# Expert tiles: the next expert's weights are rounded and split piece by piece under the last tile's products, and the gated rows go ahead of the output weights

## Chip, core and metric

The kernel runs on one core of a Trainium2 chip. The metric is the device time of one execution in microseconds (us), as the median of several runs; the profile is one further execution, recorded by the hardware profiler.

## What is computed

A block of four steps on `x` (16 sequences of 128 rows, width 512), each added to x with a `tanh` gate: a gated cross attention, a ternary linear layer, a sigmoid attention, and a mixture of experts. The change is in the last one. Cut to what matters there (T = 2048 tokens, E = 16 experts, 4 of them for each token, inner width 352):

```
_, idx = top_k(masked_scores, 4)                    # per token
cw = zeros(T, E).at[arange(T)[:, None], idx].add(w) # routing weights
h = silu(einsum('td,edh->teh', xf, w1)) * einsum('td,edh->teh', xf, w3)
y = einsum('teh,ehd,te->td', h, w2, cw)
z = silu(xf @ sw1) * (xf @ sw3) @ sw2               # shared experts
return (y + z).reshape(b, s, d)
```

## The kernel before

The steps before the experts, the routing and the shared expert fill the first 793 us and are left as they are. In `expert_tiles` the routed rows lie sorted by expert in tiles of 128 rows; 68 tiles are in use here. All engines run the same loop over trips of `UT` = 4 tiles (b = 0 to 3, n = 4 i + b). At the head of a trip each engine loads from the table `meta` whether the trip is in use and whether its first tile begins a new expert; in each tile it loads the flag of the next tile (`this, first = first, value_load(...)`). Such a load is a few register instructions and a TENSOR_LOAD in the engine's queue.

Products are made in three passes over values kept as a rounded high part (fp32r) and a low part (value minus high part). ScalarE rounds, VectorE subtracts.

TensorE, in tile n, issues in this order:
- the first products (L1925): for each of four pieces k of the width it waits for the low part of W13's piece (`w13_lo`), then six matmuls into `t_H1` and `t_H3`; the first waits for the low part of the rows, `tx_lo`;
- the transposes of the next tile's rows into `t_TX` (L1904);
- the second products of tile n-1, nine matmuls into `t_Y` (L47 to L49, `y(b)`), after waits for `th_lo` (gated rows), `w2_lo` (W2) and `y_evac`;
- the transposes of the gated rows into `t_TH` (L1937), after `hmul`.

ScalarE, in tile n: silu of `t_H1` (L1970), rounding of the next rows (L1947, `x_hi`), if the next tile has a new expert its W13 in four pieces (L1951), the output rows of tile n-1 times their routing weight (L1954, `y_out`), if this tile has a new expert its W2 in two parts (L1985, L1986), and rounding of the gated rows (L1991). VectorE: the routing weight column (L2022), the gated product (L2024), low part of the next rows (L1999, `x_lo`), W13's four splits (L2003), W2's two splits (L2039, L2042), low part of the gated rows (L2048). Where a branch for new weights isn't taken, the engine takes an Else with `drain()`, which waits until the engine is empty, and a semaphore increment in the splits' place.

W13 is one buffer: the pieces for tile n+1 overwrite those of tile n, so they can start only when tile n's products with them are through. Before the change one semaphore, `h_fill`, says so, at the end of all 24 matmuls. The raw weights have two places; SP loads the expert after the next (L1033, L1038, L1039) when a place has been split (`w13_lo`, `w2_lo`). GpSimd gathers rows (L1044) three tiles ahead and scatters the output rows with an add (L1893).

Twelve experts have rows in this input, so W13 changes eleven times inside the loop, and W2 is taken up twelve times. The tiles whose successor begins an expert are those at 801.49, 808.87, 844.27, 953.65, 988.34, 1009.77, 1037.81, 1045.81, 1101.49, 1163.03 and 1224.75 (start of L1904 in the profile).

## Time and profile before

| what | value |
|---|---|
| median of 3 runs | 1286.46 us (1286.46 to 1287.14) |
| span of the profiled execution, first to last instruction | 1286.6 us |
| TensorE matmul busy | 1210.8 us, 94% |
| VectorE busy | 676.6 us, 53% |
| ScalarE busy | 578.8 us, 45% |
| GpSimd busy | 424.5 us, 33% |
| mean granted TensorE clock | 0.986 of full speed |
| first to last tile start in the expert loop | 801.49 to 1266.07 us |
| load of half an expert's W13 (704 KB), issue to landing | 5.3 us, median |

Times in the views are in us from the start of the span. A busy share counts matmuls as they are modelled by the profiler, so 94% is no measure of the work done, but gaps in it are real. The profiled execution's only time is its span; what lies before the first and after the last instruction isn't in it.

### The profile page before, as it was taken

The numbers are of one execution on the slowest core, as the hardware profiler recorded it, in microseconds if no ns is written. First come the engines' busy times: TensorE is split into PE (matmuls) and PEld (weight loads), VectorE is DVE, ScalarE is ACT, GpSimd is POOL, SyncE is SP. The second block draws the span as 40 slices with busy tenths as digits, with TensorE's granted clock in tenths as the row PEclk, the third lists the DMA queues.
The fourth block names the chain that finished last, engine by engine and source line by source line (L and its number), as shares of the span: only waits on it lengthen the run. The fifth ranks groups of instructions, "written<-read, shape, count | busy, mean of one in ns | idle before, by whom it ended". The sixth has DMA issues, their size and how long they took to land. (4 is left out here: it accounts for less than half of the span.)

```text
span 1286.6 us, 25693 instructions
## 1 busy us (share of the span) xinstructions
PE 1210.8 (94%) x7835; PEld 1023.1 (80%) x7836; DVE 676.6 (53%) x1411; ACT 578.8 (45%) x1387; POOL 424.5 (33%) x514
## 2 busy tenths in 40 slices
PE   7998999999999879889999998999999999999995
PEld 7877777787787657667777777889999889999995
DVE  6656545545445989944576554642234552424241
ACT  5554445455356768872111112543344453434341
POOL 1102211211213656400015742244434334443443
PEclk9999999999999999989999999999999999999997
DMA  9100000000000122022000413764445766545454
GB/s 334 39 18 20 18 1 20 18 1 18 18 18 2 34 69 65 29 96 85 1 0 2 160 41 130 221 142 85 78 103 117 201 144 146 137 85 136 86 135 71
DMA packets 54335, 100.36 MB, mean 78 GB/s; under 512 B 5094, under 2 KB 21990, under 8 KB 54262
## 3 DMA queue, kind: packets, MB, share of 16 engines
q0 software_dynamic: 15824, 37.76, 15.5%
q1 hardware_dynamic: 38438, 61.65, 14.7%
q8 instruction: 43, 0.70, 0.2%
q14 instruction: 30, 0.25, 0.1%
HBM read 72.91 MB, written 26.48 MB: 77 GB/s over the span
## 5 line engine op out<-in xcount | busy, mean ns | idle before, releaser
L1925 PE MATMUL t_H<-m_W,t_xT 128*128 128x352 f32 x1632 | 281.9, 328 | 7.3 <-DVE m_W L2003 5.7
L1925 PEld LDWEIGHTS t_H<-m_W,t_xT 128*128 128x128 f32 x1632 | 263.3, 189 | 10.1 <-DVE m_W L2003 8.1
L1893 POOL DMA_INDIRECT out_dram<-t_ys,t_sid x68 | 109.5, 1610 | 225.0 <-ACT t_ys L1954 110.6
L1970 ACT ACTIVATE t_sl<-t_H 128x352 f32<-128x352 f32 x68 | 31.6, 465 | 175.6 <-PE t_H L1925 175.6
L759 ACT ACTIVATE pr<-SC,neg 128x128 f32<-128x128 f32 x256 | 90.1, 377 | 38.2 <-DVE neg L973 38.2
L47 PE MATMUL t_Y<-m_W,t_hT 128*128 128x512 f32 (+1 forms) x207 | 88.1, 426 | 4.9 <-issue 3.0
L2048 DVE TENSOR_TENSOR t_hT<-t_TH,t_hT 128x384 fp32r<-128x384 f32 x68 | 37.8, 556 | 101.8 <-ACT t_hT L1991 100.6
L2024 DVE TENSOR_TENSOR t_h<-t_H,t_sl 128x352 f32<-128x352 f32 x68 | 35.6, 523 | 104.8 <-ACT t_sl L1970 104.8
L1954 ACT ACTIVATE t_ys<-t_Y,t_wcol 128x512 f32<-128x512 f32 x69 | 47.4, 687 | 95.3 <-PE t_Y L49 95.3
L49 PE MATMUL t_Y<-m_W,t_hT 128*128 128x512 f32 (+1 forms) x207 | 82.5, 398 | 0.0
L48 PE MATMUL t_Y<-m_W,t_hT 128*128 128x512 f32 (+1 forms) x207 | 82.2, 397 | 0.0
L470 POOL TENSOR_TENSOR X<-X,upd 128x512 f32<-128x512 f32 x16 | 20.6, 1290 | 138.3 <-DVE upd L954 138.3
L697 ACT ACTIVATE pT<-T 128x512 f32<-128x512 f32 x64 | 38.5, 603 | 53.8 <-PE T L503 53.7
L970 DVE TENSOR_REDUCE mx<-SC 128x4 f32<-128x512 f32 x64 | 43.9, 686 | 33.7 <-PE SC L631 33.7
L1238 POOL TENSOR_SCALAR m_W<-m_W,bst 128x128 fp32r<-128x128 f32 x64 | 49.6, 795 | 31.4 <-PE eL L1353 31.2
L894 DVE TENSOR_TENSOR Wq<-kT,Wq 128x512 fp32r<-128x512 f32 x64 | 56.2, 902 | 3.7 <-ACT Wq L750 3.6
L440 POOL TENSOR_TENSOR tmp<-tmp,nhalf 128x2 f32<-128x2 f32 (+2 forms) x22 | 19.1, 870 | 117.3 <-DVE tmp L790 100.3
L1434 ACT ACTIVATE ehT<-eh 128x512 fp32r<-128x512 f32 (+1 forms) x24 | 15.2, 632 | 91.6 <-DVE eh L1720 91.6
L759 ACT ACTIVATION_READ_ACCUMULATOR pr<-SC,neg 128x1 f32 x256 | 55.3, 216 | 0.0
L1884 POOL COPY t_sid<-m_vals 128x1 uint32 x68 | 50.9, 748 | 0.5 <-issue 0.5
L47 PEld LDWEIGHTS t_Y<-m_W,t_hT 128*128 128x128 f32 (+1 forms) x207 | 39.4, 190 | 13.7 <-issue 5.3
L1999 DVE TENSOR_TENSOR t_xT<-t_TX,t_xT 128x512 fp32r<-128x512 f32 x69 | 47.6, 690 | 3.1 <-ACT t_xT L1947 0.3
(508 smaller groups left out, 3216.8 us busy)
## 6 DMA issues: line engine op xcount, KB each, us to landing
m_raw<-in_L_ffn_w_dram SPq DMA_DIRECT2D x28, 704.0 KB, 5.3
m_raw<-in_L_ffn_w_dram SPq DMA_DIRECT2D x14, 512.0 KB, 6.8
CT<-in_ctx_dram SPq DMA_DIRECT2D x8, 512.0 KB, 3.7
X<-in_x_dram SPq DMA_DIRECT2D x4, 1024.0 KB, 13.4
rows_d<-rows_first SPq DMA_DIRECT2D x16, 256.0 KB, 2.0
out_dram<-X SPq DMA_DIRECT2D x3, 1024.0 KB, 4.3
m_raw<-in_L_ffn_w_dram SPq DMA_DIRECT2D x14, 192.0 KB, 6.7
CT<-in_ctx_dram SPq DMA_DIRECT2D x8, 256.0 KB, 2.7
```

Source lines behind the costliest of these rows:

```text
L47: pe.matmul(out, lhs(0), rhs(0), start=first, stop=False)
L48: pe.matmul(out, lhs(0), rhs(1), start=False, stop=False)
L49: return pe.matmul(out, lhs(1), rhs(0), start=False, stop=last)
L759: i = act.activation(pr[:, t % 2, slot, :], SC[t % 2][:, slot * S:(slot + 1) * S], ACT.Exp, scale=SCALE0, bias=neg[:, t % 2, slot:slot + 1 ...
L894: dve.tensor_tensor(as_[:, n, 1, :], asg[:, n, :], as_[:, n, 0, :].bitcast(F32), ALU.subtract).then_inc(as_lo, 1)
L970: dve.tensor_reduce(mx[:, t % 2, :], bk, AX.X, ALU.max).then_inc(s_out, 1)
L1238: i = pool.tensor_scalar(tab_a[t % SLOTS][:, k, :], iP.bitcast(F32), place_p[:, t, k:k + 1], None, ALU.is_equal)
L1884: pool.tensor_copy(sid[:, b:b + 1], m["target"][:, bass.ds(n, 1)]).then_inc(zeroed, 1)
L1893: pool.indirect_dma_start(out=m["out_rows"][:, :], out_offset=bass.IndirectOffsetOnAxis(ap=sid[:, b:b + 1], axis=0), in_=ys[:, b, :], in_o ...
L1925: x_ = pe.matmul(bk[b % 2][:, 0:I], xT[:, b % 2, jx, k, :], W13[:, jw, k, j, :], start=k == 0 and jx == jw, stop=k == KC - 1 and jx == 1)
L1954: act.activation(ys[:, (b - 1) % UT, :], Y[(b - 1) % 2][:, :], ACT.Copy, scale=wcol[:, (b - 1) % UT:(b - 1) % UT + 1]).then_inc(y_evac, 1)
L1999: dve.tensor_tensor(xT[:, b % 2, 1, :, :], TX[:, :].rearrange("p (k t) -> p k t", k=KC), xT[:, b % 2, 0, :, :].bitcast(F32), ALU.subtract) ...
```

## The change

The semaphore `h_fill`, once per tile, becomes `h_part`, once per piece of the first products. ScalarE rounds pieces 0 to 2 of the next expert's W13 each behind the six matmuls that still read that piece, and only then does the gated steps (silu and rounding of the next rows, now `gated`), then piece 3. VectorE likewise: splits of pieces 0 to 2, gated product and low rows, split of piece 3. Where the next tile keeps its expert, the gated steps stand in the Else branch, ahead of its drain. Second, the rounding and the low part of the gated rows (`t_hT`) go ahead of the W2 branch on both engines, and so ahead of its drain where it isn't taken.

```diff
@@ tensor
-                            x_.then_inc(h_fill, 1)
+                                x_.then_inc(h_part, 1)
@@ scalar
+                def w13_k(k, place):
+                    act.activation(W13[:, 0, k, :, :], raw13(m, place)[:, k, :, :], ACT.Copy).then_inc(w13_hi, 1)
+                def gated(n, b):
+                    act.wait_ge(h_part, KC * n + KC)
+                    act.wait_ge(hmul, n + 1)
+                    act.activation(sl[:, :], H1[b % 2][:, 0:I], ACT.Silu).then_inc(silu, 1)
+                    act.wait_ge(tx_fill, n + 2)
+                    x_hi(b + 1)
...
-                            act.wait_ge(h_fill, n + 1)
-                            act.wait_ge(hmul, n + 1)
-                            act.activation(sl[:, :], H1[b % 2][:, 0:I], ACT.Silu).then_inc(silu, 1)
-                            act.wait_ge(tx_fill, n + 2)
-                            x_hi(b + 1)
                             with act.If(first):
                                 act.wait_ge(r13_in, 32 * (n + 2))
-                                w13(weights_at(act, m, n + 1))
+                                there = weights_at(act, m, n + 1)
+                                for k in range(KC - 1):
+                                    act.wait_ge(h_part, KC * n + k + 1)
+                                    w13_k(k, there)
+                                gated(n, b)
+                                w13_k(KC - 1, there)
                             with act.Else():
+                                gated(n, b)
                                 act.drain()
                                 act.sem_inc(w13_hi, KC)
                             act.wait_ge(y_fill, n + 1)
                             act.wait_ge(scattered, n + 1)
                             y_out(b)
+                            act.wait_ge(th_fill, n + 1)
+                            act.activation(hT[:, 0, :, :], TH[...], ACT.Copy).then_inc(th_hi, 1)
                             with act.If(this):
...
-                            act.wait_ge(th_fill, n + 1)
-                            act.activation(hT[:, 0, :, :], TH[...], ACT.Copy).then_inc(th_hi, 1)
@@ vector
+                def gated(n, b):
+                    dve.wait_ge(silu, n + 1)
+                    dve.tensor_tensor(h[:, 0:I], H3[b % 2][:, 0:I], sl[:, :], ALU.mult).then_inc(hmul, 1)
+                    dve.wait_ge(tx_hi, n + 2)
+                    x_lo(b + 1)
...
-                            dve.wait_ge(silu, n + 1)
-                            dve.tensor_tensor(h[:, 0:I], H3[b % 2][:, 0:I], sl[:, :], ALU.mult).then_inc(hmul, 1)
-                            dve.wait_ge(tx_hi, n + 2)
-                            x_lo(b + 1)
                             with dve.If(first):
                                 there = weights_at(dve, m, n + 1)
-                                for k in range(KC):
+                                for k in range(KC - 1):
                                     dve.wait_ge(w13_hi, 4 * (n + 1) + k + 1)
                                     w13_k(k, there)
+                                gated(n, b)
+                                dve.wait_ge(w13_hi, 4 * (n + 1) + KC)
+                                w13_k(KC - 1, there)
                             with dve.Else():
+                                gated(n, b)
                                 dve.drain()
                                 dve.sem_inc(w13_lo, KC)
+                            dve.wait_ge(th_hi, n + 1)
+                            dve.tensor_tensor(hT[:, 1, :, :], TH[...], hT[:, 0, :, :].bitcast(F32), ALU.subtract).then_inc(th_lo, 1)
                             with dve.If(this):
...
-                            dve.wait_ge(th_hi, n + 1)
-                            dve.tensor_tensor(hT[:, 1, :, :], TH[...], hT[:, 0, :, :].bitcast(F32), ALU.subtract).then_inc(th_lo, 1)
```

## Rows read from the trace of the kernel before

**Rows 1.** Timeline: start us, us, engine, line, operation [idle before <-releaser]; tile starts.

```profile
801.49 0.60 PE L1904 MATMUL t_TX<-identF,m_first 128*128 128x128 f32 x4
...
808.87 0.60 PE L1904 MATMUL t_TX<-identF,t_later 128*128 128x128 f32 x4
...
816.39 0.60 PE L1904 MATMUL t_TX<-identF,t_later 128*128 128x128 f32 x4
...
1266.07 0.60 PE L1904 MATMUL t_TX<-identF,m_first 128*128 128x128 f32 x4
```

**Rows 2.** Waits, 800 to 1286: waiter <- releaser: us in total, times, longest.

```profile
PEld t_H L1925 <- DVE m_W L2003: 8.1, 10, 1.3
...
PEld t_Y L47 <- issue: 5.3, 10, 3.2
...
PEld t_Y L47 <- DVE m_W L2042: 2.3, 3, 0.9
```

**Rows 3.** Timeline, an undisturbed tile with no new weights.

```profile
1142.81 0.60 PE L1904 MATMUL t_TX<-identF,t_later 128*128 128x128 f32 x4
...
1145.54 0.69 ACT L1954 ACTIVATE t_ys<-t_Y,t_wcol 128x512 f32<-128x512 f32 x1 [1.49 <-PE t_Y L49]
1145.59 4.13 PE L1925 MATMUL t_H<-m_W,t_xT 128*128 128x352 f32 x24
1146.34 0.49 ACT L1991 ACTIVATE t_hT<-t_TH 128x384 fp32r<-128x384 f32 x1
1146.87 0.56 DVE L2048 TENSOR_TENSOR t_hT<-t_TH,t_hT 128x384 fp32r<-128x384 f32 x1 [2.10 <-ACT t_hT L1991]
1147.68 0.15 DVE L2022 COPY t_wcol<-m_wgt 128x1 f32 x1 [0.26 <-issue]
...
1149.55 0.60 PE L1904 MATMUL t_TX<-identF,t_later 128*128 128x128 f32 x4
...
1149.75 0.47 ACT L1970 ACTIVATE t_sl<-t_H 128x352 f32<-128x352 f32 x1 [2.92 <-PE t_H L1925]
```

**Rows 4.** ScalarE's queue in that tile: L1988 and L1967: ns min/median/max, first, last start.

```profile
L1988 ACTq DRAIN  x1: 566/566/566, 1145.7 to 1145.7; - x1
...
L1967 ACTq SEQ_ASSERT  x1: 18/18/18, 1146.9 to 1146.9; - x1
```

**Rows 5.** Timeline, a tile whose successor has new weights.

```profile
953.65 0.60 PE L1904 MATMUL t_TX<-identF,t_later 128*128 128x128 f32 x4
...
954.29 0.60 ACT L1947 ACTIVATE t_xT<-t_TX 128x512 fp32r<-128x512 f32 x1
...
955.27 2.83 ACT L1951 ACTIVATE m_W<-m_raw 128x704 fp32r x4 [0.38 <-issue]
...
956.22 3.30 DVE L2003 TENSOR_TENSOR m_W<-m_raw,m_W 128x704 fp32r<-128x704 f32 x4 [0.61 <-ACT m_W L1951]
...
961.11 0.60 PE L1904 MATMUL t_TX<-identF,m_first 128*128 128x128 f32 x4
```

**Rows 6.** Timeline, VectorE at the head of a trip of four tiles.

```profile
1163.06 0.15 DVE L2022 COPY t_wcol<-m_wgt 128x1 f32 x1 [2.16 <-issue]
```

**Rows 7.** Timeline, W2 taken up in the last tile of a trip.

```profile
965.67 0.61 ACT L1986 ACTIVATE m_W<-m_raw 96x512 fp32r x1
...
969.40 0.15 DVE L2022 COPY t_wcol<-m_wgt 128x1 f32 x1 [1.18 <-issue]
...
969.90 0.68 DVE L1999 TENSOR_TENSOR t_xT<-t_TX,t_xT 128x512 fp32r<-128x512 f32 x1
...
970.88 0.41 PE L1925 MATMUL t_H<-m_W,t_xT 128*128 128x352 f32 x1
```

**Rows 8.** Timeline, the first trip: a load's issue and VectorE's first copy.

```profile
799.14 0.99 SPq L1033 DMA_DIRECT2D m_raw<-in_L_ffn_w_dram  x2
...
799.56 0.15 DVE L2022 COPY t_wcol<-m_wgt 128x1 f32 x1 [3.74 <-issue]
```

**Rows 9.** DMA queues, 793 to 1287: packets, MB, share of 16 engines.

```profile
q14 instruction: 4, 0.03, 0.0%
```

More of the change, by code:

```diff
@@ L1816, in expert_tiles @@
         r13_in, r2_in, w13_hi, w13_lo, w2_hi, w2_lo = (sem(f"t_{n}") for n in ("r13_in", "r2_in", "w13_hi", "w13_lo", "w2_hi", "w2_lo"))
-        tx_fill, tx_hi, tx_lo, h_fill, silu, hmul, th_fill, th_hi, th_lo, y_fill, y_evac, scattered = (
-            sem(f"t_{n}") for n in ("tx_fill", "tx_hi", "tx_lo", "h_fill", "silu", "hmul", "th_fill", "th_hi", "th_lo",
+        tx_fill, tx_hi, tx_lo, h_part, silu, hmul, th_fill, th_hi, th_lo, y_fill, y_evac, scattered = (
+            sem(f"t_{n}") for n in ("tx_fill", "tx_hi", "tx_lo", "h_part", "silu", "hmul", "th_fill", "th_hi", "th_lo",
                                     "y_fill", "y_evac", "scattered"))
@@ L1947, in x_hi @@
                     act.activation(xT[:, b % 2, 0, :, :], TX[:, :].rearrange("p (k t) -> p k t", k=KC), ACT.Copy).then_inc(tx_hi, 1)
-                def w13(place):
-                    for k in range(KC):
-                        act.activation(W13[:, 0, k, :, :], raw13(m, place)[:, k, :, :], ACT.Copy).then_inc(w13_hi, 1)
+                def w13_k(k, place):
[6 more added lines that the diff above has]
+                    x_hi(b + 1)
                 def y_out(b):
@@ L1981, in _ @@
                             y_out(b)
+                            act.wait_ge(th_fill, n + 1)
+                            act.activation(hT[:, 0, :, :], TH[:, 0:3 * P].rearrange("p (k t) -> p k t", k=3), ACT.Copy).then_inc(th_hi, 1)
                             with act.If(this):
@@ L1989, in _ @@
                                 act.sem_inc(w2_hi, 2)
-                            act.wait_ge(th_fill, n + 1)
-                            act.activation(hT[:, 0, :, :], TH[:, 0:3 * P].rearrange("p (k t) -> p k t", k=3), ACT.Copy).then_inc(th_hi, 1)
                 act.wait_ge(y_fill, trips * UT + 1)
@@ L2022, in _ @@
                             dve.tensor_copy(wcol[:, b:b + 1], wgt[:, bass.ds(n, 1)])
-                            dve.wait_ge(silu, n + 1)
-                            dve.tensor_tensor(h[:, 0:I], H3[b % 2][:, 0:I], sl[:, :], ALU.mult).then_inc(hmul, 1)
-                            dve.wait_ge(tx_hi, n + 2)
-                            x_lo(b + 1)
                             with dve.If(first):
                                 there = weights_at(dve, m, n + 1)
-                                for k in range(KC):
+                                for k in range(KC - 1):
                                     dve.wait_ge(w13_hi, 4 * (n + 1) + k + 1)
                                     w13_k(k, there)
+                                gated(n, b)
+                                dve.wait_ge(w13_hi, 4 * (n + 1) + KC)
+                                w13_k(KC - 1, there)
                             with dve.Else():
+                                gated(n, b)
                                 dve.drain()
                                 dve.sem_inc(w13_lo, KC)
+                            dve.wait_ge(th_hi, n + 1)
+                            dve.tensor_tensor(hT[:, 1, :, :], TH[:, 0:3 * P].rearrange("p (k t) -> p k t", k=3),
+                                              hT[:, 0, :, :].bitcast(F32), ALU.subtract).then_inc(th_lo, 1)
                             with dve.If(this):
@@ L2046, in _ @@
                                 dve.sem_inc(w2_lo, 2)
-                            dve.wait_ge(th_hi, n + 1)
-                            dve.tensor_tensor(hT[:, 1, :, :], TH[:, 0:3 * P].rearrange("p (k t) -> p k t", k=3),
-                                              hT[:, 0, :, :].bitcast(F32), ALU.subtract).then_inc(th_lo, 1)
 _INS = ['x', 'ctx_2048', 'mask_BxS2_bk0', 'g_xattn', 'g_ffn', 'L0_xattn_norm_w', 'L0_xattn_wq', 'L0_xattn_wk',
```

## Prediction

> **What bounds the kernel now.** I read the page's shares first (the table above): TensorE is busy nearly all of the span, so time can only come out of its gaps, or go into them. The change touches the expert tiles, the last third. There each tile starts with four transposes at L1904; 68 such starts lie between 801.49 and 1266.07 [rows 1], 67 intervals in 464.6 us. An undisturbed tile takes 1149.55 - 1142.81 = 6.74 us, product after product [rows 3]. 67 times 6.74 is 451.6, so all that can be won in this stage is 13.0 us. The view of waits says what these 13 us are [rows 2]: ten starts of the first products late by 8.1 us for the low part of the new expert's weights; three starts of the second products late by 2.3 us for W2's low part; and the "issue" row, 5.3 less the 3.2 of the very last tile, 2.1 us in nine tiles in which the low part of the gated rows came last. These sum to 12.5; the rest is two small delays.
>
> **Part 1: pieces split ahead.** Today the next expert's W13 is rounded on ScalarE after the gated rows: in the tile at 953.65 the pieces start at 955.27, VectorE follows at 956.22, the products wait for its first piece, and the tile takes 961.11 - 953.65 = 7.46 [rows 5], 0.72 over. Naively three pieces now run under the products and 8.1 us are gone. But the silu, the gated product and both halves of the next rows now stand behind three pieces in each engine's queue, and the queues are not free when the products start. I count from the start of a tile's first products (0; they end near 4.0, the next transposes are at 3.96, the next first products are due at 6.74).
>
> ScalarE: the Y rows leave at -0.05 and take 0.69 [rows 3]; the gated rows' rounding can follow at about 0.6 and ends at 1.1. Now comes a moved cost: in a tile without W2 the engine takes the branch that drains, and this drain used to lie before the gated rows (1145.7, 0.57 long [rows 4]); now it waits for their end, 1.15. Only then is the next tile's flag loaded: about 0.6, from the rows' start at 1146.34 to the assert at 1146.9 [rows 3, 4]. That gives 1.8. Branch, wait and the address of the weights took 954.29 to 955.27, 0.98, in front of the pieces [rows 5], and one more wait is added: the first piece starts at 2.8 to 2.9, though its products were through at 1.2. Pieces follow 0.68 apart (four in 2.83 [rows 5]): 2.9, 3.6, 4.25; the silu starts at 4.95 where it starts at 1149.75 - 1145.59 = 4.16 now [rows 3].
>
> VectorE: the low gated rows run 1.15 to 1.7, the drain ends at 1.75, the flag's load and the copy of the weight column take 0.81 (1146.87 to 1147.68 [rows 3]): 2.6. The address costs the same 0.8 once more: 3.4. Piece 0 is rounded at 3.7, so its split starts at 3.8; the three are 0.80 apart (four in 3.30 [rows 5]): 3.8, 4.6, 5.4. The gated product follows at 6.2, the low half of the next rows 0.43 later (969.40 copy, product right behind, 969.90 [rows 7]), ends near 7.3; the products started 0.30 after its end at 970.58 [rows 7]. So they start at 7.6, not 6.74: **0.85 over**. The stall has moved from the weights to the rows. The seven ordinary change tiles now lose about 0.7 each (0.6 to 0.8, in three of them more where a register load was stretched; that stretch stays): 7 x 0.15 = **+1.05 us**.
>
> Where the change falls on the first tile of a trip of four it is worse. There the loop head comes on top: the copy on VectorE comes at 1163.06 after 2.16 idle [rows 6], and with the 0.56 of the low gated rows it stands 2.7 after their start instead of 0.81. So it is at 4.5, the splits start at 5.45, the product at 7.85, the low rows end at 9.0, the products start at 9.25: 2.5 over against 0.6 now. This happens once after the first tile (the tile at 1163.03): **+1.9**. The tile at 808.87, which takes 816.39 - 808.87 = 7.52 now [rows 1], has W2's split of the tile before directly ahead of its pieces: W2's two splits hold VectorE to 4.2, the three pieces to 7.1, the low rows end at 8.3: 1.8 over against 0.8: **+1.0**.
>
> Gains: the very first change has long, slow products above it and nothing before it, 0.6 to about 0.1: -0.5. After two changes in a row the W2 delay at 816.39 goes (-0.6), the second change at 1045.81 finds its queues ahead because the products themselves were late (-0.45), and the tile behind it keeps half (-0.45). Sum **-2.0**.
>
> **Part 2: gated rows ahead of W2.** In a tile with W2 the chain was rounding W2, splitting W2, low gated rows; now the low gated rows run in the gap under ScalarE's W2 rounding. W2's start shifts from 0.83 to about 1.15, its last split ends at 4.2 and not the rows at 4.3, and TensorE's two waits in a row are shorter. That takes about 0.2 from six tiles: **-1.2**. In three more (for one, the tile at 967.85) the next tile heads a trip. There VectorE's copy came at 969.40, 3.73 after W2's second rounding started (965.67) [rows 7], and this start shifts by 0.35, so the low rows end at 7.1 and the products start 0.6 over against 0.25: 3 x 0.35 = **+1.05**.
>
> **Costs at nothing.** Three more semaphore signals per tile on TensorE: its matmuls are 24 in 4.13 us across today's four waits [rows 3], and the one that signals is followed as closely as the others; 0.01 us each would be 2 us, which goes to the range. In plain tiles the two drains moved and the branch now taken ahead of the silu lie in idle time: ScalarE idles 2.92 us before the silu [rows 3]. At a trip's head VectorE has the least: the copy at 1163.06 [rows 6] would come 0.5 later, when its silu's result is there, so the moved drain takes the slack but delays the gated product by less than 0.1, which has 1 us to spare. SP's loads start at other times with the splits, but are needed tiles later, but for the second change, whose load was issued at 799.14 in 0.99 us [rows 8] and, at the 5.3 to landing that the page gives for such loads, lands by 805.5, when the first piece wants it at about 807.4. GpSimd's gathers run three tiles ahead.
>
> **Sum.** 1.05 + 1.9 + 1.0 - 2.0 - 1.2 + 1.05 = +1.8 us. The profiled execution spans 1286.6, the median run is 1286.46, so they are one scale: **1288.3 us**. A measurement of this kernel can tell about 0.2%, 2.6 us, from no change; my forecast is no measurable change, on the slow side.
>
> **Rivals.**
> *A, the full gain.* If the engines stood ready at the first piece (first split at 1.9), the silu would be on time at 4.16, the low rows would end at about 6.0, and the 8.1 us would go, with 1.2 to 2.3 of Y: 1276 to 1279. The loads and drains in the rows speak against it; they would have to be overlapped, or 0.9 us shorter in each queue. Half of it would be 1282. 11%.
> The Trainium skill, Perfetto Trace Analysis, Optimizing Scalar/DVE Operations, says that where these engines aren't saturated but cause bubbles elsewhere, breaking instructions up may complete the work sooner. By that rule this rival would win; the trace agrees on the bubbles (8.1 us), but shows the pieces already separate and the queue in front of them not free.
> *B, clearly slower: the moved queue costs more.* Each of the eleven changes has two register loads more between gated rows and silu; if stretched loads or a wait order cost 0.3 us more in each, that is 3.3 us: 1291 to 1294. It decides from 0.07 us per change on, since only 0.8 us lie between my sum and the bound. For it: the path is hardly slack anywhere. Against: the usual load is short, 0.6 us with all its steps [rows 3, 4]. 22%.
> *C, code.* The loop grows by the duplicated steps. In the whole stage one instruction queue moved four packets [rows 9], all in its first 50 us, and the other one. If the longer loop were fetched anew on each trip, VectorE's head would wait as it did at first entry, 3.74 against 2.16 [rows 8, 6], 1.6 us, of which 1.0 is slack: 16 x 0.6 = 10 us, 1298. 4%.
> The Trainium skill, Advanced Engine Details and Errata, ISA Cache, gives the other engines than TensorE two lines of 256 instructions; by that rule the loop would have to pass them. No row here shows how full they are.
>
> **Chances.** Forecast 56% (four fifths of it within 0.2%), A 11%, B 22%, C 4%, the rest 7% near zero. So faster 0.13, same 0.49, slower 0.38. The range 1284.8 to 1292 leaves out A, C and the top of B.
>
> **What would show it.** Right: silu in change tiles 0.8 us later after the last product than now; the wait of the first products is for t_xT and t_h, no more for m_W; the tile at 1163 over 9 us long; W2 tiles 6.8. Wrong: first pieces starting by 1.5 us after the products do, or plain tiles other than 6.74.

## The result, and the profile after

The changed kernel takes 1291.43 us (median of 20 runs), the kernel before 1286.89 us (20 runs beside it). The ratio is 1.003, 95% interval 1.0019 to 1.004: 3.9 us slower, interval 2.4 to 5.1 (the two medians lie 4.5 apart). The forecast was 1288.3, no measurable change on the slow side, in a range of 1284.8 to 1292.0: the time is inside the range and just past the 0.2% that the forecast drew as its bound.

The page of the kernel after, its span and the shares of the engines:

```profile
span 1290.0 us, 25771 instructions
PE 1209.6 (94%) x7823; PEld 1022.8 (79%) x7836; DVE 674.8 (52%) x1411; ACT 572.0 (44%) x1387; POOL 433.1 (34%) x514
```

The waits of 800 to 1290 (waiter <- releaser: us in total, times, longest), which answer to [rows 2]:

```profile
PEld t_TH L1937 <- DVE t_h L2014: 10.0, 12, 2.9
...
PEld t_Y L47 <- issue: 3.2, 1, 3.2
PEld t_H L1925 <- DVE m_W L2010: 3.1, 3, 1.1
...
ACT m_W L1950 <- DMA m_raw<-in_L_ffn_w_dram: 2.2, 1, 2.2
```

The 8.1 us for the weights' low part are down to 3.1, and W2's 2.3 us are gone, as is what was in the "issue" row of L47 beyond the very last tile. In their place TensorE waits 10.0 us in L1937 (the transposes of the gated rows), which it did nowhere before, for the gated product, and 2.8 us more in eight starts of the first products. The stall was moved, not removed.

To see where, I took every tile's start and set each of the 67 intervals against the undisturbed 6.74 us. Before, 13.0 us lie over that; after, 18.3. "Over" stands below for the time of a tile beyond 6.74 us; a tile is named by the start of its transposes:

| tiles (their starts after) | over before | over after | difference | forecast |
|---|---|---|---|---|
| five change tiles (844.30, 953.27, 1009.66, 1037.96, 1228.21) | 4.7 | 3.0 | -1.7 | with the next row +1.05 |
| two that end a trip (988.18, 1100.05) | 1.6 | 2.6 | +1.0 | |
| the trip head 1162.01 | 0.6 | 5.5 | +4.9 | +1.9 |
| the second change 806.57 | 0.8 | 4.0 | +3.25 | +1.0 |
| the four gains | 2.8 | 0.8 | -2.0 | -2.0 |
| six tiles with W2 | 1.5 | 0.7 | -0.8 | -1.2 |
| three with W2 ahead of a trip head | 0.8 | 1.8 | +1.0 | +1.05 |
| all others | 0.3 | -0.1 | -0.3 | 0 |
| sum | 13.0 | 18.3 | +5.3 | +1.8 |

The stage began at 801.49 before and at 799.86 after; over the twelve kernels profiled here, all with the same work ahead of it, it began between 799.9 and 802.8. So 5.3 - 1.6 gives the 3.4 us between the spans within 0.3. The excess leaves out what happened ahead of the stage, but it is still that of one execution for each kernel.

**An ordinary change tile.** Timeline after, the tile that answers to [rows 5]:

```profile
949.30 4.13 PE L1925 MATMUL t_H<-m_W,t_xT 128*128 128x352 f32 x24
...
951.99 2.15 ACT L1950 ACTIVATE m_W<-m_raw 128x704 fp32r x3 [1.66 <-PE t_H L1925]
...
953.03 2.50 DVE L2010 TENSOR_TENSOR m_W<-m_raw,m_W 128x704 fp32r<-128x704 f32 x3 [1.03 <-ACT m_W L1950]
...
953.27 0.60 PE L1904 MATMUL t_TX<-identF,t_later 128*128 128x128 f32 x4
...
954.04 0.45 ACT L1955 ACTIVATE t_sl<-t_H 128x352 f32<-128x352 f32 x1
...
955.44 0.52 DVE L2014 TENSOR_TENSOR t_h<-t_H,t_sl 128x352 f32<-128x352 f32 x1
...
955.88 0.68 DVE L2006 TENSOR_TENSOR t_xT<-t_TX,t_xT 128x512 fp32r<-128x512 f32 x1
...
956.69 3.82 PE L1925 MATMUL t_H<-m_W,t_xT 128*128 128x352 f32 x22
```

Read it down the ScalarE and VectorE lines. The three pieces start at 951.99, 2.69 us after the products (949.30) although the first was free to go at about 1.2; they push the silu to 954.04, 0.77 after the transposes where 0.20 is usual. VectorE's three splits end at 955.53 and the gated product starts with their end, at 955.44; the low half of the next rows ends at 956.56, and the products start at 956.69, 3.42 after the transposes instead of 2.78.

**The trip head.** Timeline after, the tile that began at 1163.03 before:

```profile
1162.01 0.60 PE L1904 MATMUL t_TX<-identF,m_first 128*128 128x128 f32 x4
...
1162.70 2.15 ACT L1950 ACTIVATE m_W<-m_raw 128x704 fp32r x3 [3.64 <-PE t_H L1925]
...
1164.76 0.44 ACT L1955 ACTIVATE t_sl<-t_H 128x352 f32<-128x352 f32 x1
...
1166.55 0.52 DVE L2014 TENSOR_TENSOR t_h<-t_H,t_sl 128x352 f32<-128x352 f32 x1
...
1167.12 0.90 PE L1937 MATMUL t_TH<-identF,t_h 128*128 128x128 f32 x3 [2.44 <-DVE t_h L2014]
1167.80 6.61 PE L1925 MATMUL t_H<-m_W,t_xT 128*128 128x352 f32 x24
1174.25 0.60 PE L1904 MATMUL t_TX<-identF,t_later 128*128 128x128 f32 x4
```

Two losses add up: the products start 5.79 us after the transposes, 3.0 late; and then 24 products take 6.45 us to the next transposes instead of 3.96. The table of stretches says why (us, busy of PE, PEld, DVE, ACT, POOL, then PEclk, the granted clock as a share of full speed, DMA share, GB/s):

```profile
1162.00:1167.80 5.80, 3.36 (x19) 2.45 (x16) 3.82 (x7) 4.25 (x7) 1.02 (x2) 0.89 0.43 84
1167.80:1174.20 6.40, 6.40 (x26) 6.40 (x25) 1.38 (x3) 0.50 (x1) 3.46 (x4) 0.57 0.63 180
1174.20:1181.00 6.80, 6.80 (x43) 6.32 (x42) 3.27 (x5) 3.69 (x6) 2.50 (x3) 1.00 0.48 125
```

The granted clock stands at 0.57 while TensorE is busy without a gap: most of that stretch runs at the lower of its two levels, 1.2 GHz. Of the two losses, 3.0 us are the wait and 2.5 us the clock.

Part of the wait is one register load in VectorE's queue, the flag of the next tile (L2033, ns min/median/max, first and last start):

```profile
L2033 DVEq TENSOR_LOAD <-m_meta x1: 955/955/955, 1161.8 to 1161.8; - x1
```

Before the change it took 300 ns at this place. It is no accident of one execution: in all five kernels that have the gated rows ahead of W2 and the drain (after, e2, e4, e5, e9) it took 939 to 957 ns here, in the other seven 299 or 300.

**The second change.**

```profile
806.57 0.60 PE L1904 MATMUL t_TX<-identF,t_later 128*128 128x128 f32 x4
...
807.55 2.15 ACT L1950 ACTIVATE m_W<-m_raw 128x704 fp32r x3 [2.18 <-DMA m_raw<-in_L_ffn_w_dram]
809.61 0.44 ACT L1955 ACTIVATE t_sl<-t_H 128x352 f32<-128x352 f32 x1
...
811.47 0.90 PE L1937 MATMUL t_TH<-identF,t_h 128*128 128x128 f32 x3 [2.22 <-DVE t_h L2014]
812.15 5.35 PE L1925 MATMUL t_H<-m_W,t_xT 128*128 128x352 f32 x24
```

ScalarE idles 2.18 us in front of its first piece. 1.4 of them pass before the load of the weights' address begins, the step directly behind the wait for the raw weights. The silu, behind three pieces, comes 3.04 us after the transposes instead of 0.20. Here too the products run at a granted clock of 0.73 and take 5.19 us instead of 3.96. The stand cost 2.8 us, the clock 1.2.

### The profile page after: what moved, and what is told of

Read it like the earlier page. It is cut to its first block and busy times, and to the rows that moved or that the text cites. A ratio compares the mean times of both kernels' runs of the same rounds, so it can differ in the third digit from the quotient of the medians.

```text
span 1290.0 us, 25771 instructions
## 1 busy us (share of the span) xinstructions
PE 1209.6 (94%) x7823; PEld 1022.8 (79%) x7836; DVE 674.8 (52%) x1411; ACT 572.0 (44%) x1387; POOL 433.1 (34%) x514
## 3 DMA queue, kind: packets, MB, share of 16 engines
q1 hardware_dynamic: 38438, 61.65, 14.7%
## 5 line engine op out<-in xcount | busy, mean ns | idle before, releaser
L1925 PE MATMUL t_H<-m_W,t_xT 128*128 128x352 f32 x1632 | 285.6, 331 | 5.3 <-DVE m_W L2010 2.4
L1925 PEld LDWEIGHTS t_H<-m_W,t_xT 128*128 128x128 f32 x1632 | 266.9, 191 | 8.7 <-issue 4.5
L1893 POOL DMA_INDIRECT out_dram<-t_ys,t_sid x68 | 112.6, 1656 | 221.7 <-ACT t_ys L1960 147.4
L47 PE MATMUL t_Y<-m_W,t_hT 128*128 128x512 f32 (+1 forms) x207 | 88.3, 426 | 3.0 <-issue 3.0
L2034 DVE COPY t_wcol<-m_wgt 128x1 f32 x68 | 10.4, 153 | 88.9 <-issue 88.9
L1044 POOL DMA_INDIRECT m_first<-rows_d,m_pos x36 | 38.3, 1065 | 35.0 <-POOL m_pos L1885 26.6
```

The source lines that it names most:

```text
L47: pe.matmul(out, lhs(0), rhs(0), start=first, stop=False)
L1893: pool.indirect_dma_start(out=m["out_rows"][:, :], out_offset=bass.IndirectOffsetOnAxis(ap=sid[:, b:b + 1], axis=0), in_=ys[:, b, :], in_o ...
L1925: x_ = pe.matmul(bk[b % 2][:, 0:I], xT[:, b % 2, jx, k, :], W13[:, jw, k, j, :], start=k == 0 and jx == jw, stop=k == KC - 1 and jx == 1)
```

## Experiments

All but the first are edits of the changed kernel, with 5 to 12 timed runs each. "Excess" is what the 67 tiles take over 67 x 6.74 us in the profiled execution.

| kernel | pieces ahead | gated rows | ratio to before, 95% | excess | of it 2nd change | trip head |
|---|---|---|---|---|---|---|
| before | - | behind W2 | 1 | 13.0 | 0.8 | 0.6 |
| after | 3 | ahead of W2 and drain | 1.003 (1.0019 to 1.004) | 18.3 | 4.0 | 5.5 |
| e1_signals | none, old order | behind | 1.0002 (0.9993 to 1.0011) | 12.0 | 0.8 | 0.6 |
| e2_rows_alone | 0 | ahead of both | 0.9976 (0.9964 to 0.9989) | 7.7 | 0.6 | 1.15 |
| e3_pieces_alone | 3 | behind both | 0.9992 (0.998 to 1.0004) | 14.7 | 4.2 | 2.2 |
| e4_one_piece | 1 | ahead of both | 0.9947 (0.9935 to 0.996) | 6.6 | 1.4 | 1.4 |
| e5_head_late | 3, none at b = 0 | ahead of both | 1.0007 (0.9995 to 1.0019) | 15.9 | 5.5 | 1.1 |
| e9_middle_only | 3 at b = 1, 2 alone | ahead of both | 1.0016 (1.0004 to 1.0028) | 16.0 | 5.8 | 1.1 |
| e6_drain_first | 3 | ahead of W2, behind drain | 1.0007 (0.9994 to 1.0019) | 12.4 | 4.2 | 2.2 |
| e11_branch_ahead | 0 | behind both | 0.9958 (0.9945 to 0.9972) | 6.7 | 0.9 | 0.3 |
| e8_one_drain_last | 1 | behind drain, ahead of W2 but at b = 3 | 0.9941 (0.9927 to 0.9954) | 5.7 | 2.7 | 0.6 |
| e10_best | 1, none at b = 1 | as e8 | 0.9941 (0.9928 to 0.9954) | 4.7 | 0.6 | 0.6 |

The column of the second change can't be read straight down. SP issues the raw weights for it 3.1 to 3.2 us after the stage's first products start, in every kernel. In e3, e5, e8 and e9 those first products ran at a granted clock of 1.00, in the other eight at 0.69, which takes 1.5 us longer. So in e5, e8 and e9 the second change began 7.5 to 7.8 us after the issue and in the others 9.0 to 9.7, while the load took about 9: in those three it met weights that were 1.5 us later for it. (In e3 the first tile was 1.5 us over, which makes up for the clock: 9.0.) Whether an edit or chance sets the clock there, one profile for each kernel doesn't show.

### The signals alone (e1_signals)

The three more signals in each tile, with the old order everywhere else. As a diff against the kernel before:

```diff
-                            x_.then_inc(h_fill, 1)
+                                x_.then_inc(h_part, 1)
...
-                            act.wait_ge(h_fill, n + 1)
+                            act.wait_ge(h_part, KC * n + KC)
```

> The kernel before, with four signals per tile from TensorE instead of one (h_part in place of h_fill; ScalarE still waits only for the fourth). My theory (the loss comes from what stands in the queues of ScalarE and VectorE): nothing changes, undisturbed tiles stay at 6.74 us, ratio 1.000. The rival (the signals themselves cost TensorE): 3.4 to 5.3 us over 204 added signals would be 0.017 to 0.026 us each, undisturbed tiles 6.79 to 6.82, ratio 1.003.

1.0002, interval 0.9993 to 1.0011, and plain tiles of 6.74 us. The signals cost nothing that can be measured.

### The two parts by themselves (e2_rows_alone, e3_pieces_alone)

e2 keeps the gated rows ahead of W2 and puts all four pieces behind the next rows again; e3 keeps three pieces ahead and puts the rows back behind W2. In e2, on ScalarE (VectorE likewise):

```diff
-                                for k in range(KC - 1):
+                                for k in range(0):
                                     act.wait_ge(h_part, KC * n + k + 1)
...
                                 gated(n, b)
-                                w13_k(KC - 1, there)
+                                for k in range(0, KC):
+                                    w13_k(k, there)
```

In e3, gated_rows(n) being the two lines with th_fill on ScalarE and those with th_hi on VectorE:

```diff
                             y_out(b)
-                            act.wait_ge(th_fill, n + 1)
-                            act.activation(hT[:, 0, :, :], TH[:, 0:3 * P].rearrange("p (k t) -> p k t", k=3), ACT.Copy).then_inc(th_hi, 1)
...
                                 act.sem_inc(w2_hi, 2)
+                            gated_rows(n)
```

> Part 2 alone: gated rows ahead of the W2 branch, and no piece of W13 ahead of the gated steps. My theory: the ten late first products stay (8.1 us in sum), the six W2 delays of 0.25 go (-1.2), the three in front of a trip's head grow from 0.25 to about 0.55 (+1.0), the three large W2 delays shrink somewhat: -0.5 us in all, ratio 0.9995, within 0.2% of the kernel before. The rival (the gated rows' move is what makes the change slow): 3 us or more slower, ratio 1.002 or above.

> Part 1 alone: three pieces ahead of the gated steps, gated rows back behind the W2 branch, so that its drain lies ahead of them again and the next tile's flag is loaded about 0.45 us earlier. My theory: ordinary change tiles are over by 0.2 to 0.4 instead of 0.6, and the three that end a trip lose no turn of TensorE's loop (0.83 to 1.32 over in the changed kernel); the tile at a trip's head is still over by 2 us and more, the second change by 3 to 4. About -2 to +2 us against the kernel before, ratio 0.9985 to 1.0015, and 3 to 5 us faster than the changed kernel. The rival (the two parts are independent, and part 1 alone makes the loss): ratio 1.003 to 1.004 as for both.

e2 came out at 0.9976, clearly faster, where I had expected next to nothing: the change tiles had dropped from 0.6 and more to 0.21 to 0.25 over. The likely reason, which e11 puts to the test below, is an edit that I hadn't listed as one: the branch, the wait for the raw weights and the load of their address still stood ahead of the gated steps, in idle time. e3 came out level (0.9992) with an excess that is 1.7 higher: ordinary change tiles only 0.16 to 0.22 over, the silu 0.43 after the transposes and not 0.77, but the three trip ends 0.93, 0.98 and 0.72, the very first change 1.5, the second 4.2, the trip head 2.2. So each part alone is level or faster and both together slower: they aren't independent. The rows ahead of the drains cost the pieces their start.

### One piece ahead instead of three (e4_one_piece)

```diff
-                                for k in range(KC - 1):
+                                for k in range(1):
...
-                                w13_k(KC - 1, there)
+                                for k in range(1, KC):
+                                    w13_k(k, there)
```

> As the changed kernel, but only piece 0 goes ahead of the gated steps, pieces 1 to 3 behind. My theory (three pieces delay silu, gated product and next rows): the silu in ordinary change tiles is back at 0.20 us after the transposes' start, the low rows end by 6.0 of 6.74, and ordinary change tiles fall to 6.74 to 6.85; at the trip's head about 0.9 over instead of 5.5, the second change 1.3 to 2 over because its raw weights land late. Sum of what is over 6.74 in the stage about 5 us instead of 13.0 (before) and 18.3 (changed): -8 us, ratio 0.994. The rival (splits can't overlap products at all, or the branch itself costs): no better than 0.999.

0.9947, 0.8% faster than the changed kernel by the loop bound alone, as expected. Against e2, which differs from it only by having no piece ahead, it is faster too: 0.9947 against 0.9976, the intervals just apart, though the excess differs by only 1.1 us. Timeline of the same tile of the sequence:

```profile
951.33 0.79 ACT L1950 ACTIVATE m_W<-m_raw 128x704 fp32r x1 [1.65 <-PE t_H L1925]
...
952.37 0.89 DVE L2011 TENSOR_TENSOR m_W<-m_raw,m_W 128x704 fp32r<-128x704 f32 x1 [1.03 <-ACT m_W L1950]
952.62 0.60 PE L1904 MATMUL t_TX<-identF,t_later 128*128 128x128 f32 x4
952.81 0.47 ACT L1955 ACTIVATE t_sl<-t_H 128x352 f32<-128x352 f32 x1 [0.69 <-PE t_H L1925]
...
953.74 2.15 ACT L1950 ACTIVATE m_W<-m_raw 128x704 fp32r x3
...
955.39 4.13 PE L1925 MATMUL t_H<-m_W,t_xT 128*128 128x352 f32 x24
...
959.36 0.60 PE L1904 MATMUL t_TX<-identF,m_first 128*128 128x128 f32 x4
```

959.36 - 952.62 = 6.74: the change costs nothing at all in this tile. The silu is back at 0.19 after the transposes, with 0.69 us of idle left ahead of it; the split ends at 953.26, when the gated product's input is just there; and the other three pieces stay ahead of the products that use them. By these times one piece is what fits between the queue's readiness (2.7 us after the products' start) and the silu (4.16).

### Where in the trip the pieces go ahead (e5_head_late, e9_middle_only)

```diff
-                                for k in range(KC - 1):
+                                for k in range(0 if b == 0 else KC - 1):
```

e9 has `b in (0, UT - 1)` in the condition.

> As the changed kernel, three pieces ahead, but in the first tile of each trip (b = 0) all pieces stay behind the gated steps. My theory: the tile at a trip's head falls from 5.5 us over 6.74 to about 1.1, because silu and product no longer wait for pieces behind a late loop head, TensorE stands still for under 1 us there, and with it goes the stretch at half clock behind it (2.5 of the 5.5); all else as in the changed kernel, the second change still 4 over. Sum over 6.74 about 14: +1 us against before, ratio 1.001. The rival (the half clock comes on its own): products of that tile at 1.2 GHz all the same, 3 to 4 over, ratio 1.002 to 1.003.

> Three pieces ahead only in the two middle tiles of a trip (b = 1, 2), none in b = 0 and b = 3. My theory for b = 3: the late gated product holds up TensorE's queue in front of its own loop head, so the head's branch and register load are no longer hidden (1.3 over in two such tiles and 0.8 in one of the changed kernel). With none ahead there: 0.2 to 0.3 over in these three, though the tiles behind lose 0.4 to 1.2 as in the run of the rows alone; in sum -0.7 us against the run with only the head late, ratio 1.0005. The rival (these tiles are long for the weights, not for the loop): the first products there still start at 3.5 to 4.1 after the transposes.

In e5 the trip head falls from 5.5 to 1.1 over. Its silu and products in the timeline, then the stretch of the whole tile:

```profile
1167.01 0.47 ACT L1955 ACTIVATE t_sl<-t_H 128x352 f32<-128x352 f32 x1 [3.60 <-PE t_H L1925]
...
1170.26 4.10 PE L1925 MATMUL t_H<-m_W,t_xT 128*128 128x352 f32 x24 [0.85 <-DVE m_W L2011]
```

```profile
1166.30:1174.30 8.00, 7.15 (x43) 6.32 (x42) 5.10 (x9) 4.62 (x8) 3.22 (x4) 1.00 0.33 66
```

The granted clock is 1.00 throughout: without the long stand the slow products are gone as well. e9 shows the other place. Its tile at 993.08 is the trip end that lost 1.27 us in the kernel after:

```profile
993.08 0.60 PE L1904 MATMUL t_TX<-identF,m_first 128*128 128x128 f32 x4
...
996.08 4.14 PE L1925 MATMUL t_H<-m_W,t_xT 128*128 128x352 f32 x24
...
1000.06 0.60 PE L1904 MATMUL t_TX<-identF,m_first 128*128 128x128 f32 x4
```

6.98 us, 0.24 over. Against it, the kernel after:

```profile
988.18 0.60 PE L1904 MATMUL t_TX<-identF,m_first 128*128 128x128 f32 x4
...
990.66 0.68 DVE L2006 TENSOR_TENSOR t_xT<-t_TX,t_xT 128x512 fp32r<-128x512 f32 x1
990.80 0.55 PE L1937 MATMUL t_TH<-identF,t_h 128*128 128x128 f32 x3
992.24 0.42 PE L1925 MATMUL t_H<-m_W,t_xT 128*128 128x352 f32 x1 [0.90 <-DVE m_W L2010]
```

The low half of the next rows was ready at 991.34, and the weights' first three pieces before it; still the products began at 992.24. The wait is put down to VectorE's weights, which had long been done. TensorE's own queue shows what it was (L1916, the loop head's flag, 989 to 993; ns min/median/max, first and last start):

```profile
L1916 PEldq TENSOR_LOAD <-m_meta x1: 302/302/302, 991.3 to 991.3; - x1
```

The queue stood at the wait for the gated product until 990.80; only behind it could it branch to the next trip and load its flags. With the product on time this loop head runs while earlier matmuls are still being worked off: in all 16 trips of the kernel before this load starts 1.7 or 1.8 us after the transposes, here 3.1. But neither e5 nor e9 is faster than the kernel before. The second change is worse in both (5.5 and 5.8): it is b = 1, where both keep three pieces behind the load's wait, and both belong to the executions in which the weights came later for it. And e9 won nothing over e5, where I had expected 0.7 us: its three trip ends lose 0.2 each, 2.7 us less together, but the tiles behind them lose 2.6 more, 1.8 of it at one place (1056.34).

### The drain ahead of the rows (e6_drain_first)

Three pieces ahead; the gated rows go ahead of W2 where W2 is taken up, and behind the drain where it isn't.

```diff
-                            act.wait_ge(th_fill, n + 1)
-                            act.activation(hT[:, 0, :, :], TH[:, 0:3 * P].rearrange("p (k t) -> p k t", k=3), ACT.Copy).then_inc(th_hi, 1)
                             with act.If(this):
+                                gated_rows(n)
...
                                 act.sem_inc(w2_hi, 2)
+                                gated_rows(n)
```

> As the changed kernel, three pieces ahead, but where W2 isn't taken up the drain and its increment stand ahead of the gated rows again; the gated rows are ahead of W2 only where W2 is taken up. My theory (the moved drain delays the next tile's flag load by 0.45): silu in ordinary change tiles at 0.42 as in the run of the pieces alone instead of 0.77, these tiles 0.15 to 0.2 over instead of 0.5 to 0.66, the trip's head about 2.2 over, no W2 delay of 0.25. Sum over 6.74 about 11 to 12, -1.5 us against before, ratio 0.999. The rival (the drain's place is of no account): silu stays at 0.77, ratio 1.003.

1.0007 against the changed kernel's 1.003, excess 12.4 against 18.3. Timeline:

```profile
953.31 0.60 PE L1904 MATMUL t_TX<-identF,t_later 128*128 128x128 f32 x4
953.74 0.45 ACT L1955 ACTIVATE t_sl<-t_H 128x352 f32<-128x352 f32 x1
...
956.28 3.95 PE L1925 MATMUL t_H<-m_W,t_xT 128*128 128x352 f32 x23
```

The silu comes 0.43 after the transposes instead of 0.77, the products at 2.97 instead of 3.42. The moved drain was 0.45 of the 0.6 us of each ordinary change tile, and through the trip head (2.2 instead of 5.5) the largest single part of the loss: there TensorE stood 1.63 us in front of the gated rows' transposes instead of 2.44, and its products ran at a clock of 1.00. The 0.8 us are not the drain's time alone, because the register load of 955 ns took 300 here (another one, of the weights' address, took 589). The expected ratio was 0.999; its 12.4 us of excess are just over the 11 to 12 forecast.

### The branch and the address ahead, nothing else (e11_branch_ahead)

No piece ahead and the rows behind W2 and the drains, as before the change: only the branch, the wait for the raw weights and the load of their address stay ahead of the silu. Against the kernel before, on ScalarE (VectorE likewise, and the Else branch begins with the same gated steps):

```diff
-                            act.wait_ge(h_fill, n + 1)
-                            act.wait_ge(hmul, n + 1)
-                            act.activation(sl[:, :], H1[b % 2][:, 0:I], ACT.Silu).then_inc(silu, 1)
-                            act.wait_ge(tx_fill, n + 2)
-                            x_hi(b + 1)
                             with act.If(first):
                                 act.wait_ge(r13_in, 32 * (n + 2))
-                                w13(weights_at(act, m, n + 1))
+                                there = weights_at(act, m, n + 1)
+                                gated(n, b)
+                                for k in range(0, KC):
+                                    w13_k(k, there)
```

> Only one thing of the change: the branch on a new expert, with the wait for its raw weights and the load of their place, stands ahead of the gated steps, and all four pieces behind them; gated rows behind the W2 branch as before. It asks what made the run of the rows alone 0.24% faster. Theory 1 (the place's load of 0.6 us has moved into idle time, so the pieces start right behind the next rows): ordinary change tiles 0.23 over instead of 0.6 to 1.3, the W2 delays of 0.25 and 0.6 to 0.9 as before, sum over 6.74 about 7 instead of 13.0: -6 us, ratio 0.9955. Theory 2 (the gain came from the gated rows' move): change tiles 0.6 to 1.3 over as before, ratio 1.000.

```profile
952.94 0.60 PE L1904 MATMUL t_TX<-identF,t_later 128*128 128x128 f32 x4
953.57 0.60 ACT L1947 ACTIVATE t_xT<-t_TX 128x512 fp32r<-128x512 f32 x1
954.07 2.82 ACT L1950 ACTIVATE m_W<-m_raw 128x704 fp32r x4
...
955.94 4.12 PE L1925 MATMUL t_H<-m_W,t_xT 128*128 128x352 f32 x24
```

0.9958, as expected. From the high rows to the first piece it is 0.50 us, where it was 0.98 [rows 5], and the tile is 0.22 over instead of 0.72. So of what the faster kernels win, most is this hoist: 6.3 us of excess, against 6.4 for e4, which loses elsewhere what its piece wins. Beside e2, which differs by the place of the rows alone, e11 has 1.0 us less excess: the rows ahead of W2 save 0.25 in six tiles, and pay it back in the three tiles ahead of a trip head (0.53 to 0.55 against 0.21 to 0.29), at the trip head (1.15 against 0.33) and in two tiles behind a trip end (0.45 and 0.41 against nothing and 0.06). In the ratios the intervals of the two overlap, and so do those of e11 and e4: that a piece ahead adds to the hoist is shown beside e2 and not beside e11.

### The best version (e8_one_drain_last, e10_best)

One piece ahead; the drain first; W2 behind the rows, except in the last tile of a trip. Against e4, on ScalarE (VectorE likewise; gated_rows as in e3):

```diff
                             y_out(b)
-                            act.wait_ge(th_fill, n + 1)
-                            act.activation(hT[:, 0, :, :], TH[:, 0:3 * P].rearrange("p (k t) -> p k t", k=3), ACT.Copy).then_inc(th_hi, 1)
                             with act.If(this):
+                                if b < UT - 1:
+                                    gated_rows(n)
...
+                                if b == UT - 1:
+                                    gated_rows(n)
                             with act.Else():
                                 act.drain()
                                 act.sem_inc(w2_hi, 2)
+                                gated_rows(n)
```

e10 moreover lets nothing go ahead at b = 1, where the second change falls:

```diff
-                                for k in range(1):
+                                for k in range(0 if b == 1 else 1):
```

> Built from what the runs showed: one piece ahead of the gated steps; the drain ahead of the gated rows where W2 isn't taken up; the gated rows ahead of W2 where it is, but behind it in the last tile of a trip, whose successor has a late loop head. My theory: ordinary change tiles at 6.74 as with one piece, the trip's head 0.4 to 0.9 over instead of 1.4, the three tiles after a W2 at a trip's end 0.25 over instead of 0.5, the second change still 1.4 over. Sum over 6.74 about 4.5 to 5.5: -8 us against before, ratio 0.9935. The rival (one piece with the changed kernel's row order is already all there is): ratio 0.995 as that run.

> As the last one, but in the second tile of a trip (b = 1) no piece stands ahead of the gated steps. It holds the second change of the kernel, whose raw weights land late and whose queues still hold W2. My theory: that tile falls from 1.4 over to about 0.6, one later change in such a tile (near 1220) goes from 0 to 0.23, all else the same: 0.5 us faster than the last one, ratio 0.993. The rival (the landing alone sets that tile): it stays at 1.4, ratio as the last one.

Both 0.9941, about 7.6 us faster than the kernel before and 0.9% faster than the changed one. The second change shows what e10 is for. In e8:

```profile
811.95 0.79 ACT L1950 ACTIVATE m_W<-m_raw 128x704 fp32r x1 [3.50 <-DMA m_raw<-in_L_ffn_w_dram]
812.64 0.44 ACT L1955 ACTIVATE t_sl<-t_H 128x352 f32<-128x352 f32 x1
```

In e10:

```profile
807.97 0.60 PE L1904 MATMUL t_TX<-identF,t_later 128*128 128x128 f32 x4
...
808.67 0.47 ACT L1955 ACTIVATE t_sl<-t_H 128x352 f32<-128x352 f32 x1 [1.75 <-PE t_H L1925]
```

The tile's excess is 2.7 in e8 and 0.6 in e10, but the two executions differ by more than the edit: in e8 the tile began 7.5 us after the weights were issued, in e10 9.1. The fair comparison is e4, with one piece ahead and 9.0 us after the issue: 1.4, so the edit is worth about 0.8 there. That is the fall that was expected, and the rival (the landing alone sets the tile) is refuted: the wait stands ahead of the silu in e10 as well. In the ratio nothing of it shows, whose intervals are 3.5 us wide. Which of the two is better stays open, as does how much of e8's edits beyond e4's (0.9947, overlapping intervals) is worth its lines.

## Why the prediction was nearly right, and where it failed

**Held.** The main step did: the queues aren't free when the products start, and a stall for weights becomes a stall for rows. Term by term in an ordinary tile, from the products' start: first piece forecast at 2.8 to 2.9, measured 2.69; first split 3.8 and 3.73; gated product 6.2 and 6.14; end of the low rows 7.3 and 7.26; products 7.6 and 7.39. The three tiles ahead of trip heads (+1.05 and +1.0), the signals (e1) and plain tiles at 6.74 us (no sign of code fetched anew, rival C) came as forecast. The six tiles with W2 gave 0.8 of 1.2. Rival A fell by the same step; e6 and e4 show its condition in part: with the drain back, or one piece only, the loss shrinks or is gone.

**Right by luck: the four gains, -2.0 and -2.0.** Term by term they were -0.5, -0.6, -0.45 and -0.45; measured -0.7, -0.7, +0.2 and -0.9. The change at 1045 ends a trip and lost instead of gaining, and the tile behind it lost all its delay and not half.

**Mis-sized: "0.85 over".** It was 0.6. I took 0.30 us from the end of the low rows to the products from [rows 7]. But there the products didn't wait for the rows: TensorE was still at its own matmuls, the transposes of the gated rows at 970.63 directly ahead. Where the rows come last it is 0.13. This and 0.08 us of the rest made five tiles 1.2 us cheaper than forecast.

**Failed: "that stretch stays".** It went. Two of these five were 1.28 and 1.26 over before, with an address load of the weights that took 1009 ns on VectorE and one of 837 ns on ScalarE; after, with these loads ahead of the silu, they take 280 to 313 ns in both tiles, and the tiles are 0.6 over like the rest. That is another 1.2 us. The five tiles were forecast at +0.75 and came at -1.7.

**Failed: the trip end, which I priced as ordinary.** The rivals asked for stretched loads on ScalarE and VectorE; the load that counted was in TensorE's queue, which has to pass its own loop head behind the wait for the gated product: 0.90 us from the low rows' end to the products instead of 0.13. e9 shows it by leaving those tiles alone: 0.24 over instead of 1.27. Two tiles, 1.4 us more than at the ordinary five's price, and the change at 1045 besides.

**Failed: the trip head, "+1.9", measured +4.9.** 3.0 less the 0.6 of before is 2.4 us of stand, near my 1.9; VectorE's flag load, 0.955 us long instead of 0.30, is more than the difference. The 2.5 us on top are the products at the lower clock, a term that the sum didn't have. e5 takes the stand away, e3 and e6 shorten it to 1.6 us, and in all three the clock stays at 1.00.

**Failed: "lands by 805.5, when the first piece wants it at about 807.4".** From the issue at 799.14 that allowed 6.4 us. In the kernel after, the load was issued at 797.50, and ScalarE stood at its wait until the load of the address, the step behind it, could start:

```profile
L1027 ACTq TENSOR_LOAD <-m_meta x1: 277/277/277, 806.9 to 806.9; - x1
```

That is 9.4 us; in the five others in which the profile puts ScalarE's wait down to this load (e4, e5, e6, e8 and e9) it is 9.2 to 9.6. The 5.3 us, a median over all such loads, were no bound for this one, which runs while the DMA engines are at least 0.66 busy (799 to 805); that this is the cause wasn't tested. So VectorE's first split came at 808.49, about 1 us after its own queue was ready, the stand grew to 2.8 us over instead of 1.8, and the clock added 1.2: +3.25 instead of +1.0. What makes the late load dear is what stands behind its wait. e2 and e10 keep the wait ahead of the silu but have no pieces there: the silu comes 0.29 and 0.70 after the transposes instead of 3.04, the tile is 0.60 and 0.64 over.

**What the forecast didn't look for.** It counted branch and address as a cost ahead of the pieces (0.98 and 0.8 us) and never asked what hoisting them alone would do. e11 says 5.4 us gained.

So the sign came from the step forecast (a stall moved), and the size did not. Ordinary change tiles even gained 1.7 us; the loss is at three kinds of place that multiply a late product: trip end, trip head and second change, +9.1 us together where the forecast had +3.2. That the time stayed inside the range is partly luck: without the 2.4 us by which the five ordinary tiles undercut their price it would have come near 1294. The clearly slower rival had the sign and the size, and not the mechanism: nothing cost 0.3 us more in each change.

The Trainium skill, Perfetto Trace Analysis, Optimizing Scalar/DVE Operations, says that breaking up instructions may complete work sooner where these engines aren't saturated but make others idle. No run here breaks an instruction up further; what they try is starting pieces that are already separate sooner. That agrees for one piece (0.9947 against 0.9976 for none, e4 and e2) and not for three (1.003): at 44 and 52% busy the engines aren't saturated, but what was due next stood behind the pieces in the same queue.

**Open.** What makes the clock fall. In the twelve profiles TensorE stood six times for 2.06 to 3.09 us in front of the gated rows' transposes (the second change of after, e3, e5, e6 and e9, the trip head of after), and each time the next products ran at a granted 0.57 to 0.74. After three stands of 1.64, 1.63 and 1.92 us (the trip heads of e3 and e6, the second change of e8) they ran at 1.00. But the stage's first products, all after 1.5 us of idle, ran at 0.69 in eight kernels and at 1.00 in four. No run varies the stand by itself, so this is what was seen and no rule. Why some register loads take 0.6 to 1.1 us instead of 0.3 is open too; they return at the same places in kernels with the same order. One in TensorE's loop head, of 976 ns, goes with the tile at 1242.18, which should have gained 0.25 and lost 0.4. In e3, e5, e6 and e9, which also have three pieces ahead there, it takes 912 to 1117 ns, in the kernels with fewer about 300.

## What to carry to other kernels

Before work is sliced and put ahead in an in-order queue, find when that queue is really free, and move only as many slices as end before the next due instruction; here one of three was right, 0.5% faster against 0.3% slower. Hoist what needs no data first, the branch and the address: that alone gave 5.4 of the best version's 7.6 us. Leave the drain where it doesn't wait for late work. A wait for a transfer, with the work that hangs on it, shouldn't come to stand ahead of work that doesn't need it, and a producer that comes late at the end of a loop body is paid twice, because the consumer's own loop head is no longer hidden.

## What the runs showed of the hardware that was not expected

TensorE's granted clock fell to 0.57 and 0.73 in the stretch right after a stand of 2.4 and 2.2 us, and was 1.00 again in the tile behind; products took 6.45 and 5.19 us instead of 3.96. A queue's register load from memory takes 0.27 to 0.31 us as a rule and at times 0.6 to 1.1. And TensorE's loop head, hidden as long as matmuls are queued ahead of it, costs 0.8 us when they aren't (0.90 us from the low rows' end to the products instead of 0.13).
